# A flamingo block on one core: the steps of ACT, DVE and POOL in another order, TensorE's as it was

## The reference

```python
x = x + tanh(g_xattn) * xattn(layernorm(x), ctx, ctx, Wq, Wk, Wv, Wo, qpos, kpos, mask)
x = x + tanh(g_ffn) * ffn(layernorm(x), Wr, Wk, Wv, mu_r, mu_k)

# xattn: scores = Q K^T / sqrt(32) - slope[head] * (qpos - kpos), masked
m = max(scores); e = exp(scores - m); attn = e / (1 + sum(e)); out = (attn V) Wo^T
# ffn: x_prev is x moved on by one token
r = sigmoid((mu_r * x + (1 - mu_r) * x_prev) Wr^T)
k = (mu_k * x + (1 - mu_k) * x_prev) Wk^T
out = r * (relu(k)**2 Wv^T)
```

## Time and profile before

| what | value |
|---|---|
| median of three runs | 1474.18 us (1472.98 to 1476.51) |
| the profiled execution, its own time | 1474.89 us |
| its span in the profile | 1473.1 us |
| busy: PE, DVE, ACT, POOL | 1372.3, 1128.0, 891.0, 720.5 us |
| granted TensorE clock, in tenths of full speed | 9 (90% or more) in each of the 40 slices |
| transfers, mean over the span | 45 GB/s |

### The profile page before, as it was taken

One profiled execution on the slowest core, in us unless ns is written; L12 is line 12 of the kernel. 1 busy time (PEld: TensorE's weight loads), 2 busy tenths in 40 slices (PEclk: granted clock), 3 DMA queues, 4 the chain that ended last, 5 costly groups with the idle time before them and its releaser, 6 DMA issues.

```text
span 1473.1 us, 34107 instructions
## 1 busy us (share of the span) xinstructions
PE 1372.3 (93%) x11584; PEld 1143.7 (78%) x11584; DVE 1128.0 (77%) x2745; ACT 891.0 (60%) x2928; POOL 720.5 (49%) x766
## 2 busy tenths in 40 slices
PE   7988999999999999999999999999999999999988
PEld 6876778778787877878787787878787787878767
DVE  5447868787887878788786879878687878878675
ACT  5247475665747476674747566574756657474752
POOL 0003555645555554555555465545556455555542
PEclk9999999999999999999999999999999999999999
DMA  8721002020100102011010201111010201101000
GB/s 270 220 80 38 26 17 64 0 53 26 49 29 28 50 0 79 0 49 29 28 50 14 64 0 49 29 40 39 28 51 0 64 15 49 29 28 42 3 29 29
DMA packets 53010, 65.97 MB, mean 45 GB/s; under 512 B 23024, under 2 KB 29168, under 8 KB 52976
## 3 DMA queue, kind: packets, MB, share of 16 engines
q1 hardware_dynamic: 52976, 65.52, 14.9%
HBM read 40.87 MB, written 24.64 MB: 44 GB/s over the span
## 4 chain that ended last, share of the span: by engine, by line
PE 36%; DVE 28%; issue 17%; POOL 9%; ACT 6%; DMA 2%; DVEq 1%; SPq 0%; POOLq 0%; ACTq 0%
PE rotating L417 26%; DVE diff L1144 4%; DVE probs_room L1082 4%; DVE mix_k L1136 4%; POOL probs_room L1362 4%; PE score_bank L417 3%; PE probs_bank L584 3%; ACT probs_room L824 3%; POOL norm L1400 2%; DVE relu L1144 2%; PE attn_bank L598 2%; DVE stats L1049 2%; DVE norm L1061 2%; DVE xs L1105 2%; POOL mixed_gate L1395 1%
## 5 line engine op out<-in xcount | busy, mean ns | idle before, releaser
L824 ACT ACTIVATE probs_room<-probs_room 128x121 f32<-128x121 f32 x1024 | 392.1, 388 | 28.5 <-DVE probs_room L1086 28.5
L1362 POOL TENSOR_TENSOR probs_room<-probs_room,recip 128x960 f32<-128x960 f32 x128 | 229.7, 1795 | 209.4 <-DVE recip L1094 209.4
L417 PE MATMUL rotating<-w_proj,attn_t 128*128 128x512 f32 x768 | 207.6, 409 | 21.0 <-ACT gated L875 19.0
L1082 DVE SCALAR_TENSOR_TENSOR probs_room<-mask_in,score_bank 128x120 f32<-128x120 f32 x1024 | 212.9, 270 | 3.3 <-issue 0.3
L417 PE MATMUL rotating<-mixed_key,w_key 128*128 128x256 f32 x1440 | 198.5, 289 | 11.0 <-ACT gated L875 11.0
L417 PE MATMUL rotating<-w_value,xnt_or_act 128*128 128x512 f32 x720 | 202.7, 410 | 6.4 <-DVE xs L1105 6.4
L831 ACT COPY probs_room<-probs_bank 120x512 f32<-120x512 f32 x256 | 150.0, 586 | 82.0 <-PE probs_bank L584 80.4
L417 PE MATMUL rotating<-xnt_or_act,w_query 128*128 128x256 f32 x1536 | 198.8, 286 | 0.5 <-DVE xnt_or_act L1067 0.5
L417 PEld LDWEIGHTS rotating<-mixed_key,w_key 128*128 128x128 f32 x1440 | 178.6, 191 | 22.0 <-ACT gated L875 17.3
L824 ACT ACTIVATION_READ_ACCUMULATOR probs_room<-probs_room 128x1 f32 x1024 | 195.0, 190 | 0.0
L417 PEld LDWEIGHTS rotating<-xnt_or_act,w_query 128*128 128x128 f32 x1536 | 187.8, 191 | 1.9 <-DVE xnt_or_act L1067 0.8
(11 more groups left out here) (121 smaller groups left out, 2109.7 us busy)
## 6 DMA issues: line engine op xcount, KB each, us to landing
xs<-in_x_dram SPq DMA_DIRECT2D x64, 256.0 KB, 2.9
out_dram<-gated SPq DMA_DIRECT2D x64, 256.0 KB, 3.0
value_scratch<-gated SPq DMA_DIRECT2D x16, 240.0 KB, 2.7
mask_in<-in_mask_dram SPq DMA_DIRECT2D x16, 240.0 KB, 3.3
keys_t<-key_scratch SPq DMA_DIRECT2D x16, 240.0 KB, 2.6
values<-value_scratch SPq DMA_DIRECT2D x16, 240.0 KB, 4.2
probs_room<-in_ctx_t_dram SPq DMA_DIRECT2D x6, 480.0 KB, 7.4
key_scratch<-query_t SPq DMA_DIRECT2D x12, 240.0 KB, 4.9
```

Source lines behind the costliest of these rows:

```text
L417: mm = pe.matmul(bank, stationary(a, c), moving(b, c), start=(i == 0), stop=(i == MATMULS - 1))
L824: e = act.activation(row, row, ACT.Exp, bias=neg_max[:, t % 2, head:head + 1], scale=-1.0, accum_out=sums[:, t % 2, head:head + 1])
L1082: z = dve.scalar_tensor_tensor(out=probs[:, t % 2, head, :], in0=far, scalar=-SLOPES[head], in1=score_banks[j][:, g * NK:(g + 1) * NK], op ...
L1362: pool.tensor_tensor(part, part, recip[:, t % 2, heads].unsqueeze(2).to_broadcast((P, H // 2, NK)), ALU.mult)\
```

## The change

The order of the steps in three of the four hand-written streams of a batch is written anew: in `batch` of ACT, DVE and POOL. TensorE's stream and SP's stay as they are; no step is added, removed or altered. The same text serves the first, the middle and the last batches.

```diff
@@ -911,39 +911,39 @@
 front, back = range(J // 2), range(J // 2, J)
 feed_forward((gate_out, 0))
 exps(b, 0, 0)
+exps(b, 0, 1)
 feed_forward((gate_out, 1))
-exps(b, 0, 1)
 exps(b, 0, 2)
 feed_forward((relu_out, 0))
 exps(b, 0, 3)
 feed_forward((act_split, 0))
-feed_forward((relu_out, 1))
 probs_out(b, 0, 0)
 probs_out(b, 0, 1)
+probs_out(b, 0, 2)
+feed_forward((relu_out, 1))
+probs_out(b, 0, 3)
 feed_forward((act_split, 1))
-probs_out(b, 0, 2)
-probs_out(b, 0, 3)
 feed_forward((relu_out, 2))
 attn_out(b, 0)
 exps(b, 1, 0)
-feed_forward((act_split, 2))
-feed_forward((relu_out, 3))
 exps(b, 1, 1, front)
-feed_forward((act_split, 3))
 exps(b, 1, 1, back)
 exps(b, 1, 2)
+feed_forward((relu_out, 3))
 exps(b, 1, 3)
+feed_forward((act_split, 2))
+exps(b, 2, 0, front)
 probs_out(b, 1, 0)
 probs_out(b, 1, 1)
-exps(b, 2, 0, front)
 probs_out(b, 1, 2)
 exps(b, 2, 0, back)
 probs_out(b, 1, 3)
-attn_out(b, 1)
 exps(b, 2, 1)
 exps(b, 2, 2)
+attn_out(b, 1)
 exps(b, 2, 3)
 feed_forward((gate_out, 2))
+feed_forward((act_split, 3))
 turn2_out(b, 0)
 exps(b, 3, 0)
 probs_out(b, 2, 0)
@@ -956,17 +956,17 @@
 exps(b, 3, 2, back)
 attn_out(b, 2)
 exps(b, 3, 3)
+probs_out(b, 3, 0)
 feed_forward((gate_out, 3))
-probs_out(b, 3, 0)
+probs_out(b, 3, 1)
 after((turn1_out, 0))
-probs_out(b, 3, 1)
-turn2_out(b, 1)
 probs_out(b, 3, 2)
 mix_key_high(b, 0)
+turn2_out(b, 1)
 probs_out(b, 3, 3)
+after((turn1_out, 1))
+attn_out(b, 3)
 mix_gate_high(b, 0)
-attn_out(b, 3)
-after((turn1_out, 1))
 after((turn1_out, 2))
 after((query_out, 0))
 turn2_out(b, 2)
@@ -977,8 +977,8 @@
 turn2_out(b, 3)
 after((query_out, 2))
 mix_key_high(b, 2)
+after((query_out, 3))
 mix_gate_high(b, 2)
-after((query_out, 3))
 mix_key_high(b, 3)
 mix_gate_high(b, 3)

@@ -1211,56 +1211,56 @@
 bias(b, 1, 2)
 bias(b, 1, 3)
 attn_low(b, 0)
+bias(b, 2, 0)
+bias(b, 2, 1)
+reciprocals(b, 1, 0)
+bias(b, 2, 2)
+residual(b, 0)
+statistics2(b, 0)
+reciprocals(b, 1, 1)
+feed_forward((finish, 0))
 if not last:
     distances(b + 1)
-reciprocals(b, 1, 0)
-bias(b, 2, 0)
-residual(b, 0)
-reciprocals(b, 1, 1)
-bias(b, 2, 1)
-bias(b, 2, 2)
 bias(b, 2, 3)
-statistics2(b, 0)
-feed_forward((finish, 0))
 normalise2(b, 0)
+feed_forward((finish, 1))
+reciprocals(b, 2, 0)
+bias(b, 3, 0)
 attn_low(b, 1)
-reciprocals(b, 2, 0)
-feed_forward((finish, 1))
 after((statistics1, 0))
 reciprocals(b, 2, 1)
-bias(b, 3, 0)
 bias(b, 3, 1)
-after((normalise1, 0))
 bias(b, 3, 2)
 residual(b, 1)
+bias(b, 3, 3)
+reciprocals(b, 3, 0)
 statistics2(b, 1)
-reciprocals(b, 3, 0)
-bias(b, 3, 3)
+after((statistics1, 1))
+after((normalise1, 0))
+normalise2(b, 1)
 feed_forward((finish, 2))
-normalise2(b, 1)
 attn_low(b, 2)
-after((statistics1, 1))
 reciprocals(b, 3, 1)
 mix_key(b, 0)
-mix_gate(b, 0)
 after((turn1_low, 0))
 after((normalise1, 1))
+residual(b, 2)
+mix_gate(b, 0)
 after((statistics1, 2))
-residual(b, 2)
+after((turn1_low, 1))
 attn_low(b, 3)
-after((turn1_low, 1))
-after((normalise1, 2))
 statistics2(b, 2)
 feed_forward((finish, 3))
+after((normalise1, 2))
 normalise2(b, 2)
 residual(b, 3)
+mix_key(b, 1)
 after((turn1_low, 2))
 after((statistics1, 3))
 statistics2(b, 3)
 after((normalise1, 3))
 normalise2(b, 3)
 after((turn1_low, 3))
-mix_key(b, 1)
 mix_gate(b, 1)
 mix_key(b, 2)
 mix_gate(b, 2)
@@ -1424,27 +1424,27 @@
 feed_forward((squared_relu, 1))
 feed_forward((act_rest, 1))
 feed_forward((squared_relu, 2))
+normalise_probs(b, 1, 0)
 feed_forward((squared_relu, 3))
-feed_forward((act_rest, 2))
-feed_forward((act_rest, 3))
-normalise_probs(b, 1, 0)
 normalise_probs(b, 1, 1)
 rstd2_of(b, 0)
 normalise_probs(b, 2, 0)
-after((rstd1_of, 0))
+feed_forward((act_rest, 2))
+feed_forward((act_rest, 3))
 normalise_probs(b, 2, 1)
 edge(b, 0)
 difference(b, 0)
+after((rstd1_of, 0))
+normalise_probs(b, 3, 0)
 rstd2_of(b, 1)
-normalise_probs(b, 3, 0)
 normalise_probs(b, 3, 1)
 after((rstd1_of, 1))
-edge(b, 1)
-difference(b, 1)
 after((rstd1_of, 2))
 mix_key_low(b, 0)
+edge(b, 1)
+rstd2_of(b, 2)
+difference(b, 1)
 mix_gate_low(b, 0)
-rstd2_of(b, 2)
 after((rstd1_of, 3))
 rstd2_of(b, 3)
 edge(b, 2)
@@ -1453,8 +1453,8 @@
 mix_gate_low(b, 1)
 edge(b, 3)
 difference(b, 3)
+mix_gate_low(b, 2)
 mix_key_low(b, 2)
-mix_gate_low(b, 2)
 mix_key_low(b, 3)
 mix_gate_low(b, 3)
             for t in range(QT):
```

## The result

The changed kernel takes 1448.68 us in the median of four runs (1447.49 to 1450.2), the kernel before 1473.58 beside it. The ratio is 0.983, interval 0.981 to 0.985: 24.9 us faster, where 21.6 was forecast.

What follows compares the result with a forecast made beforehand. TensorE bounds the kernel; only its idle gaps, 4.7 us a batch, can be won. Legs of 43.00 + 23.10 + 17.07 give 83.17 us, 1.43 less per batch; 21.6 us in all, so 1453 us, own range 1443 to 1463.

Steps and rivals of the forecast that it cites:

- the limit of 4.7 us: TensorE's idle gaps per batch: no reordering of the other engines can gain more than 4.7 us a batch.
- Leg A: Third probability transposition of tile 0 to last attention product: 44.32 us before, 43.00 forecast.
- The copy's gap: TensorE's 0.70 us wait per batch for a probability copy on ACT; forecast to go.
- the late scaling of tile 1: Tile 1's reciprocals stand behind tile 2's bias groups, so POOL's scaling is late: new gap of 0.25 us.
- The distances in the busy stretch: DVE's distances move ahead of tile 2's last bias; 0.6 us cover before scores 3, without it up to 1.0 cost.
- Leg B: Last attention product to the next first gate product: 22.36 us before, 23.10 forecast.
- The two new gaps: Before transpositions 2 and 3 of the normalised input, POOL blocking DVE's normalisations: 1.2 us together.
- Leg C: First gate product to third probability transposition of tile 0: 17.92 us before, 17.07 forecast, first bias at 4.35 instead of 5.20.
- Its two reasons: One key mix less at DVE's end; ACT's last query copy ahead of the third gate mix's copy, delaying POOL's last conversions.
- The faster one: Rival, chance 0.17: DVE wins the port at normalisations or ends its last mix before POOL's conversions; 1433 to 1436, down to 1425.
- the slower one: Rival, chance 0.20: POOL idles some 6 us, then all three long instructions block DVE's normalisations; 1478 to 1490 us.
- the one in which little is gained: Rival, chance 0.13: POOL's conversions catch the third key mix, bias starts at 5.4, leg C gives nothing; 1463 to 1478 us.

Runs made afterwards that it cites:

- the last run: Changed kernel plus a POOL wait (except last batch), POOL's tile 1 difference early, and tile 1's second reciprocals earlier on DVE: 1405.82 us, ratio 0.953 to the kernel before.
- Undoing two ACT edits: Two runs of the changed kernel: relu 1 and split 1 put back on ACT, 1460.09 us; attention 1's high part ahead of the exponentials again, 1466.92 us.
- the run with the early difference: Changed kernel with POOL's edge and difference of tile 1 ahead of its wait for statistics 2, and gate conversion 0 later: 1445.58 us.
- the end of the batch: Changed kernel with the old order of ACT's third gate mix copy and POOL's tile 2 conversions at the batch's end: 1446.88 us.
- the wait on POOL: Changed kernel with one wait added: POOL's last four conversions of a batch start only after DVE's last gate mix: 1426.52 us; same wait in the kernel before: 1432.52 us.

## Why the prediction was right

**The bound.** It was right in the main that TensorE's gaps are what can be won, and that a gap adds up with about its own size. TensorE's idle time fell from 4.72 to 3.30 us a batch, 1.42 of the 1.55 won. So the limit of 4.7 us was a little low: the last run won 4.51 and still has 0.52 of idle time a batch. Undoing two ACT edits gave back 0.75 and 0.95 us a batch, where the earlier trace rows showed gaps of 0.70 and 1.27 - 0.33 = 0.94.

**Leg A.** 43.03 measured, 43.00 forecast. The copy's gap went, the tanh's fell to 0.33 (0.40 forecast), and the late scaling of tile 1 costs 0.33 (0.25). The distances in the busy stretch cost nothing: no wait for scores 3 appears.

**Leg B.** 23.14 measured, 23.10 forecast. The two new gaps are 0.48 and 0.60, together 1.08 for the 1.2 forecast, at the transpositions and with the releaser that were named. DVE's normalisations took 1.26 and 1.50, so 0.72 and 0.96 us more than free, for 0.77 and 1.0. That POOL's instructions do it is shown by the run with the early difference, where both are free and both gaps gone. That POOL would be ahead at both places no row of before showed; the prediction had to choose there, and said so, so this part of the hit is luck.

**Leg C.** 16.90 measured, 17.07 forecast; the bias came at 4.17 for 4.35. Its two reasons fared differently. The key mix that moved ahead is why the bias comes earlier here: undone, it starts at 5.19. That this gain is mostly paid for in leg B, so that the move is worth 0.22 us net, the run with the key mix put back shows; the prediction counted the mix in both legs, but did not set the two against each other. The query copy ahead of the third mix's copy does set where POOL's conversions begin, but it decides nothing: in the old order the bias comes 0.15 us sooner.

**The sum.** 1.43 us a batch were forecast, 1.55 measured, over fourteen periods 21.6 us for 20.0 (by the score products, 1162.8 for 1184.4 us). From the last batch's second scores to the end there are 100.8 us for 102.7 before, 1.9 less, where 1.6 was forecast. Before the first steady batch the changed kernel is 1.2 us earlier, where nothing was forecast; its first scores start 1.1 us later (96.92 us for 95.78; in all these profiles they lie between 93.6 and 96.9), so the way from there to the second batch's second scores is some 2.3 us shorter, of which about 1.0 is leg C's. One profile of each can't say more. 21.6 + 1.9 + 1.2 is the 24.7 us between the spans.

**The rivals.** The faster one, DVE winning the port, did not happen: POOL's instruction had started 0.28 and 0.24 us ahead at both places. Of the slower one the idle time and the backlog are there, but only two of three instructions blocked; the key conversion (737.57, 1.30) ran beside low halves and a `finish`, which read PSUM, and the statistics, none of them longer than before.

Of the one in which little is gained the condition came true and its consequence did not. The third key mix was caught, 3.22 us for 1.13 (750.61). But the third gate mix behind it took 1.81 where the kernel before has 3.89:

```profile
764.98 3.89 DVE L1144 SCALAR_TENSOR_TENSOR diff<-diff,mu,xn2t 128x128 f32<-128x128 f32 x4
```

DVE's mixes begin 7.24 us before the first gate product in both kernels (749.56 to 756.80, 760.54 to 767.78), and what they take beyond 1.13 each is 5.9 us in the changed kernel and 5.8 before. POOL holds them up for as long as it did; the bias comes 1.03 us earlier because one key mix fewer stands there.

If the parts add, the undone ones account, of the gain of 1.55 us a batch, for 0.75 + 0.95 + 0.22 - 0.15 = 1.77 (the copy, the tanh, the key mix, the end of the batch). The rest of the new order, which was not taken apart, then loses about 0.2 on balance: the residual's gap of 0.46 won, the late scaling's 0.33 lost, and the two new gaps at the normalisations lost, as far as the key mix does not already account for them.

## What to carry to other kernels

When a hand-written order is judged, follow one batch step by step between fixed points of the full engine and give each step the time from its start to the next step's start in the trace; the sum of the gaps told the time here within 0.3%. Where two engines hold each other up, as DVE and POOL do here, what matters is not only the order on each but what the other one starts meanwhile: one wait that keeps POOL still while DVE is on the critical path was worth 41 us, more than the reordering of three engines. And the order of the loop is also run in the first and the last batch: look at what the tail needs first before moving a step back.

## What the runs showed of the hardware that was not expected

- Closing a gap of TensorE wins a little more than the gap: with the wait on POOL the gaps of 0.77 and 0.80 us went (1.57), and the period fell by 1.64. The three gaps that the wait closed in the kernel before are 2.27 us, with 0.1 less at the copy, and the period fell by 2.81. Where the rest lies is not shown.
- A DVE multiply-add that waits for POOL gets through at each boundary of two POOL instructions, one at a time: of the last mix's four the first ran ahead of POOL's three conversions (756.99 to 760.90), and the other three ended 0.15 us after each of these, so that the mix took 4.29 us.
